# Graph attention and routed experts on one core: routing of four graphs in six parts, a second PSUM bank for V, and a new order of the drain

## What is computed

```python
def attention(x, adj):                       # on layernorm(x)
    q, k, v = x @ Wq.T, x @ Wk.T, x @ Wv.T   # 16 heads of 32
    p = softmax(q @ k.T * D ** -0.5 + adj + adj)
    return (p @ v) @ Wo.T

def experts(x):                              # on layernorm(x): 8 experts of 512 x 512, the best 2 count
    scores = maximum(x @ gate_W + gate_b, 1e-4)
    p = softmax(scores); top = top_k(p, 2)
    w = maximum(p, 0.1); w = w / w[top].sum(); comb = where(in_top, w, 0)
    return einsum(x @ expert_W + expert_b, comb) / 2

x = x + attention(layernorm(x), adj)
x = x + experts(layernorm(x))
```

## Time and profile before

| | |
|---|---|
| median of 3 runs | 1660.67 us (1660.43 to 1661.73) |
| the profiled execution | 1662.81 us; span from first to last instruction 1661.0 |
| PE busy | 1550.8 us, 93% |
| PEld busy | 1410.9 us, 85% |
| DVE busy | 1215.8 us, 73% |
| ACT busy | 955.9 us, 58% |
| POOL busy | 974.0 us, 59% |
| mean granted TensorE clock | 0.970 |

### The profile page before, as it was taken

The page is one execution under the profiler, slowest core; times in us unless marked ns, Lnnn a source line. Parts: engine busy times, 40 slices in busy tenths (PEclk is TensorE's granted clock), DMA queues, the critical chain, the costliest instruction groups (busy, mean ns, idle before and its releaser), DMA issues. The chain is left out here.

```text
span 1661.0 us, 45460 instructions
## 1 busy us (share of the span) xinstructions
PE 1550.8 (93%) x12808; PEld 1410.9 (85%) x12808; DVE 1215.8 (73%) x4952; ACT 955.9 (58%) x3129; POOL 974.0 (59%) x1788
## 2 busy tenths in 40 slices
PE   6999999999999999999999999966189999999996
PEld 6999999999999999999999999955167777777775
DVE  5578888888888888888888788877745555555554
ACT  4687777777777777777777777775111111111111
POOL 3255666566666666566665666556235565565655
PEclk9999999999999999999999999977599999999998
DMA  6787988789888888888887888794658898898886
GB/s 226 194 233 199 257 241 241 237 248 253 246 241 240 244 247 239 237 239 247 228 244 225 246 233 228 221 293 142 217 102 158 168 174 164 162 169 165 164 160 106
DMA packets 188629, 351.98 MB, mean 212 GB/s; under 512 B 20960, under 2 KB 30304, under 8 KB 188256
## 3 DMA queue, kind: packets, MB, share of 16 engines
q1 hardware_dynamic: 135520, 238.47, 51.7%
q0 software_dynamic: 29680, 69.55, 21.6%
q10 hardware_dynamic: 23184, 41.05, 8.0%
HBM read 189.48 MB, written 159.52 MB: 210 GB/s over the span
## 5 line engine op out<-in xcount | busy, mean ns | idle before, releaser
L678 ACT ACTIVATE prob<-prob,nmax 128x128 f32<-128x128 f32 x1024 | 398.8, 395 | 175.3 <-DVE amax L833 168.8
L1146 POOL TENSOR_TENSOR prob<-prob,rinv 128x512 f32<-128x512 f32 x256 | 261.4, 1042 | 241.3 <-DVE rinv L850 241.2
L829 DVE CUSTOM_DVE_ANT_0 prob<-ps_s,bias 128x128 f32<-128x128 f32 x1024 | 237.7, 287 | 142.1 <-PE ps_s L530 106.5
L1343 POOL DMA_INDIRECT out<-yt,token x135 | 211.6, 1567 | 196.3 <-DMA out<-yt,token 72.3
L1281 ACT ACTIVATE xgT_hi<-ps_x 128x512 fp32r<-128x512 f32 x135 | 80.7, 598 | 386.8 <-PE ps_x L1266 339.4
L1260 PE MATMUL ps_y<-we,xgT_hi 128*128 x540 | 260.8, 483 | 5.8 <-DVE xgT_lo L1300 5.8
L1261 PE MATMUL ps_y<-we,xgT_hi 128*128 x540 | 214.8, 398 | 0.0
L1262 PE MATMUL ps_y<-we,xgT_lo 128*128 x540 | 214.0, 396 | 0.0
L678 ACT ACTIVATION_READ_ACCUMULATOR prob<-prob,nmax 128x1 f32 x1024 | 196.7, 192 | 0.0
L833 DVE TENSOR_REDUCE amax<-prob 128x4 f32<-128x512 f32 x256 | 175.6, 686 | 8.9
L539 PE MATMUL ps_t<-const,prob 128*128 128x128 f32 x1024 | 164.8, 284 | 15.2 <-ACT pT L716 12.1
(11 more groups left out here) (191 smaller groups left out, 4770.4 us busy)
## 6 DMA issues: line engine op xcount, KB each, us to landing
ks<-kq_parts SPq DMA_DIRECT2D x192, 256.0 KB, 4.2
qs<-kq_parts SPq DMA_DIRECT2D x192, 256.0 KB, 6.3
xg<-x_lists ACTq DMA_DIRECT2D x135, 260.5 KB
xin<-x SPq DMA_DIRECT2D x64, 256.0 KB, 7.2
kq_parts<-kT_hi SPq DMA_DIRECT2D x32, 512.0 KB, 3.8
kq_parts<-kT_lo SPq DMA_DIRECT2D x32, 512.0 KB, 4.8
kq_parts<-qT_hi SPq DMA_DIRECT2D x32, 512.0 KB
kq_parts<-qT_lo SPq DMA_DIRECT2D x32, 512.0 KB
```

Of the source, the lines that this page charges most:

```text
L678: last = nc.scalar.activation(prob[:, r, c, h, :], prob[:, r, c, h, :], ACT.Exp, bias=nmax[:, r, i:i + 1], scale=-1.0, accum_out=rsum[:, r ...
L829: last = nc.vector.tensor_tensor_reduce(out=prob[:, r, c, h, :], in0=ps_s[c % 2][:, P * h:P * h + P], in1=bias[:, b % 4, :], scale=-1.0, s ...
L1146: tt(prob[:, r, q], prob[:, r, q], rinv[:, r, HC * q:HC * q + HC].unsqueeze(2).to_broadcast([P, HC, P]), ALU.mult)\
L1343: pool.indirect_dma_start(out=out, out_offset=bass.IndirectOffsetOnAxis(ap=token[:, m, :], axis=0), in_=yt[:, r, :], in_offset=None, compu ...
```

## The change

Routing goes by groups of four graphs (the last eight graphs by pairs). For group b to b + 3 the chain is cut in six parts on VectorE: scores (11 instructions) and first choice (4) at steps 0 and 2 of turn b + 7; second choice (7) at step 0 of turn b + 8; weigh (8) and combine (4) at steps 0 and 2 of turn b + 9; find (6) at step 0 of turn b + 10. ScalarE's eexp stands in turn b + 8, TensorE's counting, now eight matmuls for four graphs, at step 1 of turn b + 9. Graph b + a is scattered in turn b + 10 + a. V's right half of the pair's first graph goes to ps_o, of the second to ps_g. xn2 gets eight slots, gate_x six. In the drain the high and low parts of the experts stand elsewhere, GpSimd makes the statistics of graph 61 behind the last normalise and oT_lo, four pieces are left behind the table, and fourteen are made by VectorE in phase two, behind the low part of its second tile; TensorE waits for the pieces of its first three tiles by a value read from memory.

The diff, cut to its core:

```diff
+LATE = 18
...
+GROUPS = [(4 * q, 4) for q in range((B - 8) // 4)] + [(b, 2) for b in range(B - 8, B, 2)]
+STEPS = ("scores", "first", "second", "place", "exp", "weigh", "combine", "find")
...
+def plan():
+    at = {n: {} for n in STEPS}
+    for g, (b, n) in enumerate(GROUPS):
+        t = b + n
+        if n == 4 and GROUPS[g + 1][1] == 4:
+            when = (t + 3, 0), (t + 3, 2), (t + 4, 0), (t + 5, 1), (t + 4, 0), (t + 5, 0), (t + 5, 2), (t + 6, 0)
+        else:
+            when = (t + 2, 3), (t + 3, 0), (t + 3, 0), (t + 3, 2), (t + 3, 1), (t + 3, 2), (t + 4, 0), (t + 4, 0)
...
+        first_need = sb(top, "first_need", [1, RING], i32)
...
-        gate_x = sb("gate_x", [P, 8, E])
+        gate_x = sb("gate_x", [P, 6, E])
-        xn2 = sb("xn2", [P, 4, W])
+        xn2 = sb("xn2", [P, 8, W])
+        all_one = xn2[:, 0, 0:P]
-        pos = sb("pos", [P, 2, K, 2], i32)
+        pos = sb("pos", [P, 3, K, 4], i32)
...
-        G_V, G_P = ps_g[:, 0:D // 2 + E], ps_g[:, 3 * P:3 * P + 3 * E]
+        G_V, G_P = [ps_o[:, 0:D // 2 + E], ps_g[:, 0:D // 2 + E]], ps_g[:, 3 * P:3 * P + 5 * E]
-        O_W, O_S = ps_o[:, 0:DC * E], ps_o[:, DC * E:DC * E + E]
+        O_W, O_S = ps_t[:, 0:DC * E], ps_t[:, DC * E:DC * E + E]
...
-        HI_AT = [(B - 2, 1), (B - 2, 2), (B - 1, 1), (B - 1, 2), (B, 2), (B + 1, 3), (B + 3, 0), (B + 3, 1)]
-        LO_AT = {0: (B, 0), 1: (B, 2), 2: (B + 1, 0), 3: (B + 2, 0), 4: (B + 2, 2), 5: (B + 3, 0)}
+        HI_AT = [(B - 2, 1), (B - 2, 2), (B - 1, 1), (B + 1, 0), (B + 1, 2), (B + 2, 2), (B + 3, 0), (B + 3, 1)]
+        LO_AT = {(B - 1, 3): 2, (B, 0): 4, (B, 1): 2, (B + 2, 1): 6}
...
-                    if 2 * n + part:
-                        pe.wait_ge(v_done, 2 * n + part)
-                    if part == 0 and okp((t - 6) // 2):
-                        pe.wait_ge(place_step, PLACE * ((t - 6) // 2) + 1)
+                    if part == 0 and ok(t - 2):
+                        pe.wait_ge(oT_done, t - 1)
+                    if part == 1 and n >= 1:
+                        pe.wait_ge(v_done, 2 * n)
+                    if part == 1 and any(w < (t, c) for w in AT["place"]):
+                        pe.wait_ge(place_step, PLACE * max(g for w, g in AT["place"].items() if w < (t, c)) + 1)
...
+                    if b % 2 and ok(b + 3):
+                        pe.wait_ge(v_done, b + 4)
...
+            def places(g, t):
+                first, n = GROUPS[g]
+                pe.wait_ge(route_step, ROUTE * g + 16)
+                pe.wait_ge(v_done, min(B, t + 3))
...
+                mm(rows(G_P, 0, n + 1), tri[:, :], rows(sums, 0, n + 1), start=True, stop=False)
+                for i in range(1, n):
+                    mm(rows(G_P, i + 1, n + 1), ones[:, :], rows(sums, 1, n + 1 - i), start=False, stop=False)
+                for i in range(n):
+                    last = mm(rows(G_P, 0, 1), ones[:, :], rows(sums, i + 1, i + 2), start=False, stop=i == n - 1)
+                last.then_inc(place_full, 1)
...
-                    if b >= 8:
-                        act.wait_ge(x1_done, b - 7)
+                    if b >= 6:
+                        act.wait_ge(x1_done, b - 5)
...
-                if b >= 4:
-                    act.wait_ge(scattered[b % 4], 32 * (b // 4))
+                if b >= 8:
+                    act.wait_ge(scattered[b % 8], 32 * (b // 8))
...
+            def experts_lo(pieces):
+                for _ in range(pieces):
+                    e, i = divmod(made[0], DC)
+                    made[0] += 1
+                    dve.wait_ge(we_hi_done, e + 1)
                     own = slice(D * i, D * i + D)
                     tt(expert(e, 1)[:, own], expert(e, 1)[:, own].bitcast(f32), expert(e, 0)[:, own].bitcast(f32), ALU.subtract).then_inc(we_lo_done, 1)
...
+            ts(first_need[:, :], tab_f[:, 0, 0:RING], float(DC), float(DC), ALU.mult, ALU.add)
             link(nc.vector.tensor_copy(tab[:, :, :], tab_f[:, :, :]))
-            for e in range(len(LO_AT), E):
-                expert_lo(e)
+            experts_lo(LATE - made[0])
...
-                    if c == 0 and not odd and ok(t - 3):
+                    if c == 0 and not odd and ok(t - 3) and t < B:
                         second_rstd(t - 3)
...
                         tt(oT_lo[:, :, :], oT[:, :, :], oT_hi[:, :, :].bitcast(f32), ALU.subtract).then_inc(oT_lo_done, 1)
+                    if c == 0 and not odd and ok(t - 3) and t >= B:
+                        second_rstd(t - 3)
...
-                    if c == (3 - 2 * a if t < B else 3) and okp(p):
-                        scatter(p, a)
+                    if c == (3 if t >= B or not odd else 1):
+                        for b in range(B):
+                            g, a = GROUP_OF[b]
+                            if t == FOUND[g][0] + a:
+                                scatter(b)
...
+                        if not t.after(R):
+                            need = pe.value_load(v["first_need"][0:1, bass.ds(t.count(), 1)], min_val=DC, max_val=DC * E)
+                            pe.wait_ge(v["we_lo_done"], need)
...
+                    if (g, j) == (0, 0):
+                        for e, i in (divmod(piece, DC) for piece in range(LATE, DC * E)):
+                            hi, lo = (we[:, (2 * e + part) * DC * D + D * i:(2 * e + part) * DC * D + D * i + D] for part in range(2))
+                            tt(lo, lo.bitcast(f32), hi.bitcast(f32), ALU.subtract).then_inc(v["we_lo_done"], 1)
```

More of the change, by code:

```diff
@@ L49 @@
 C_ALL = C_DUM + E
+GROUPS = [(4 * q, 4) for q in range((B - 8) // 4)] + [(b, 2) for b in range(B - 8, B, 2)]
[8 more added lines that the diff above has]
+            when = (t + 2, 3), (t + 3, 0), (t + 3, 0), (t + 3, 2), (t + 3, 1), (t + 3, 2), (t + 4, 0), (t + 4, 0)
+        for name, w in zip(STEPS, when):
+            at[name][w] = g
+    return at
+AT = plan()
+FOUND = {g: w for w, g in AT["find"].items()}
+GROUP_OF = {b + a: (g, a) for g, (b, n) in enumerate(GROUPS) for a in range(n)}
 class Item:
@@ new lines, in landed, with combine @@
+            def landed(graphs):
+                for b in graphs:
+                    dve.wait_ge(scattered[b % 8], 32 * (b // 8 + 1))
+            def combine(g):
+                first, n = GROUPS[g]
+                link = chain(ROUTE * g, 22, route_step)
+                link(nc.vector.scalar_tensor_tensor(out=wgt[:, :, 0:n], in0=wgt[:, :, 0:n], scalar=1.0 / K,
+                                                    in1=wtot[:, 0:n].unsqueeze(1).to_broadcast([P, K, n]), op0=ALU.mult, op1=ALU.mult))
+                link(tt(comb_k[:, :, 0:n, :], mask[:, :, 0:n, :], wgt[:, :, 0:n].unsqueeze(3).to_broadcast([P, K, n, E]), ALU.mult))
+                landed(range(max(0, first - 8), first - 8 + n))
+                k = first % 8
+                tt(xn2[:, k:k + n, D + 1:W], comb_k[:, 0, 0:n], comb_k[:, 1, 0:n], ALU.add)
+                link(nc.vector.tensor_copy(xn2[:, k:k + n, D], const[:, C_TOK + first:C_TOK + first + n]))
@@ new lines, in find_places @@
+            def find_places(g):
+                _, n = GROUPS[g]
+                link = chain(PLACE * g, 0, place_step)
+                r = g % 3
+                old, new = fill[:, g % 2, :], fill[:, 1 - g % 2, :]
+                places = G_P.rearrange("p (a e) -> p a e", a=5)
+                dve.wait_ge(place_full, g + 1)
+                tt(place[:, 0:n, :], places[:, 1:n + 1, :], old.unsqueeze(1).to_broadcast([P, n, E]), ALU.add)
+                link(tt(new, places[:, 0, :], old, ALU.add))
@@ L1015, in _ @@
                         first_stats(t + 4 + c)
-                    p = (t - 6) // 2
-                    if not odd and okp(p):
-                        if c == 1:
-                            weigh(p)
-                            find_places(p)
-                    p = (t - 5) // 2
-                    if odd and okp(p):
-                        if c == 2:
-                            gate_scores(p)
-                        if c == 3:
-                            choose(p)
-                    for e, at in LO_AT.items():
-                        if at == (t, c):
-                            expert_lo(e)
-            dve.wait_ge(place_step, PLACE * (B // 2))
+                    if (t, c) in AT["scores"]:
+                        gate_scores(AT["scores"][t, c])
+                    if (t, c) in AT["first"]:
+                        choose_first(AT["first"][t, c])
+                    if (t, c) in AT["second"]:
+                        choose_second(AT["second"][t, c])
+                    if (t, c) in AT["weigh"]:
+                        weigh(AT["weigh"][t, c])
+                    if (t, c) in AT["combine"]:
+                        combine(AT["combine"][t, c])
+                    if (t, c) in AT["find"]:
+                        find_places(AT["find"][t, c])
+                    experts_lo(LO_AT.get((t, c), 0))
+            dve.wait_ge(place_step, PLACE * len(GROUPS))
```

224 lines of the change are left out of this document (100 added, 124 removed).

## The result

The changed kernel takes 1650.22 us (median of four runs, 1648.90 to 1650.76), the kernel before beside it 1660.55: ratio 0.9924, 95% interval 0.9912 to 0.9936. It is faster, but by a third of what I forecast: 1650.2 against 1630.3, outside my range of 1620 to 1648. The profiled execution has a span of 1649.0 us and 1650.75 in all, beside 1661.0 and 1662.8 before, so the two traces differ by 12.0.

The account below looks back on a forecast made before the run. TensorE's own work order was taken to bound 61 turns, so only its delays count. Terms -28.1 (turns), +1.5, +2.3, -6.5, -2.2, +2.6 sum to -30.4 us: 1630.3 against 1660.7, range 1620 to 1648.

Parts of the forecast that it names:

- A lump of four at step 0 of the odd turn: VectorE's longest routing part, 11 instructions, 2.1 us, fits a 4.9 us step beside 1.6 of maxima and 0.4 of reciprocals.
- the port rule: Drain: GpSimd and two-SBUF-input VectorE instructions exclude each other; the term to the last positions would then be -4.5 us.
- half of the gain: Rival, chance 0.16: VectorE's load slips in odd turns, output projection waits for the residual sum; 14 of 28 us, 1644.3.
- The even turns and the routing matmuls: Even turns fall to 16.9 to 17.0 us; eight routing matmuls add about 0.3 in every other odd turn.
- A bank for each graph: Even turns: separate banks for V's right halves remove V's second wait, 0.22 us for the copy out of ps_g.
- the 1.16 us: Price of routing per pair of turns on TensorE's path; taken back whole in 28 even turns, 32.4 us.
- The drain: GpSimd's new order delays ScalarE's xn of graph 61, then pT to the residual of graph 63: +2.3 us, bounds -2 and +5.
- To the last positions: From graph 63's residual to the last positions, six pieces and combine and find ahead: 14.6 us instead of 21.1, -6.5.
- Behind the table: End of phase one: VectorE makes four pieces there instead of eight: -2.2 us, bounds 0 and -2.4.
- Fourteen pieces: Phase two, ahead of the third xgT_lo: 8.6 us of pieces, partly in idle time, delay the first yt: +2.6, bounds 0 and +6.
- The end of the attention: Last scores: doubled late scatters lengthen the DMA queue ahead of graph 63's Q parts: +1.5 us, bounds 0 and 3.6.
- The slower rival, V in ps_o: Rival, chance 0.04: odd turn's product waits for ScalarE's copy out of ps_o, 2.7 us a pair, 81 us, 1711.

Follow-up runs that it names:

- run 1: Changed kernel with the 'scores' part of a group of four at step 1 of the even turn, not step 0 of the odd: 1642.6 us, ratio 0.9865.
- run 3: Changed kernel with the score tile of the groups of four in free columns of ps_g (PSUM) instead of SBUF: 1641.31 us, ratio 0.9866.
- Run 4: Changed kernel with the bank part alone undone, both right halves of V in ps_g again: 1649.98 us, ratio 0.9927.
- Run 6: Changed kernel with GpSimd's old order in the drain, second_rstd ahead of normalise and oT_lo: 1645.71 us, ratio 0.9891.
- run 10: Changed kernel with 'scores' at step 1 of the even turn, GpSimd's old drain order and LATE = 32, no piece in phase two: 1641.65 us, ratio 0.9882.
- run 11: The changed kernel measured again, unaltered: 1649.38 us, ratio 0.9913.

## Why the prediction was wrong

The direction and the mechanism of the gain were right, the size was not. By its own steps:

*A lump of four at step 0 of the odd turn: the step that failed.* "The longest lump, 11 instructions (2.1 us), stands at step 0 of an odd turn ...: it fits." It took 4.6. Count and step price were right: away from GpSimd the part takes 1.97 us (run 1), and with its scores in PSUM 2.01 (run 3). What I put at nothing was the overlap with GpSimd's products, 2.6 us. I priced the chain by comb_k, 192 ns, which stands after GpSimd's products. In the same view stood the warning (VectorE by line, 200 to 1000 us, of the kernel before; busy, mean ns of one):
```profile
L929 DVE TENSOR_TENSOR em<-eexp,mask 128x16 f32<-128x16 f32 x23 | 13.1, 568 | 0.0
```
half the size of comb_k, three times as long: it stood beside oT_lo and ended with it (at 598.29 and 598.26 in turn 32). I brought the port rule in for the drain and never asked what GpSimd does at each of the places the parts were moved to. What followed is the wait of my rival "half of the gain", to which I gave 0.16: the output projection waits for the sum with the residual. That rival named lack of room, not GpSimd, as the reason, and it priced 14 us. Runs 1 and 3 put the waits at 0.67 us in every other pair, 8.8 us over 26 pairs. The pair without them, 33.21 against 33.17, is 1.1 more; the last 0.6 of the 10.5 lies in the first and last groups (my 28.1 also counts the pair of turn 60, which the stretch to turn 60 does not) and was not taken apart.

*The even turns and the routing matmuls* were right: 16.97 us, and 0.28 in every other odd turn. *A bank for each graph* I credited with a part of the 1.16 us. Run 4 shows that it brings nothing beside the new routing.

*The drain*, +2.3 with a bound of +5, measured +4.9. The chain I named is the one that happened. The term was mis-sized: xn of graph 61 came 14.4 us behind its residual where I had 11.4. Half of that is second_rstd, which took 5.0 us beside VectorE's six pieces and not 3.5; I had taken stretched steps into account for graph 63 alone. The rest is normalise of graph 63, which started 6.1 us behind that residual and not 4.3 (GpSimd stood 1.01 us for VectorE's rinv), though it was 0.5 shorter. Run 6 gives this part of the loss as 3.7.

*To the last positions*, -6.5, measured -5.4: between the sum and what I wrote for the port rule, -4.5. VectorE waits 0.82 us for off of graph 63 behind its pieces.

*Behind the table*, -2.2, measured +0.2, just outside my bound of 0. Before, the first load came 1.0 us behind VectorE's last piece; after, 3.5 us behind it. With VectorE out of the way another chain ended phase one: the load comes 15.4 to 16.2 us behind the last positions in every run with LATE up to 23, against 15.3 before. SyncE, after its DMAs, stands 2.9 us more for TensorE's sequencer, and I had counted only the landing of the last scatter. That wait names no cause: in run 10, where VectorE's pieces end the phase, the same wait is 9.2 us, so the sequencer may pass on the lateness of another engine. What sets the 15.4 us was not tried.

*Fourteen pieces*, +2.6, measured +2.3: the room of six microseconds was right (ten pieces free, run 10), the closeness of the sum is in part luck. The pieces cost 1.7; the other 0.6 stands without any piece. The value reads of first_need, which I put at nothing, are the likely cause, not a tested one.

*The end of the attention*, +1.5, measured +0.1: two executions of the changed kernel differ by 1.5 us in this stretch (run 11), so one profile of each kernel cannot tell +0.1 from +1.5. Whether the doubled scatters hold up the last loads stays open.

The gap of 18.4 us between the sum and the traces is 10.5 in the turns, 2.5 at the start, 2.6 and 1.1 in the drain, 2.4 behind the table and 0.9 at the end, less 1.4 and 0.3. The slower rival, V in ps_o, did not show: no wait for that copy in any turn.

## What to carry to other kernels

When work is moved on VectorE, look at GpSimd's timeline at the new place before pricing it: an instruction of 0.2 us took up to 1.1 there. Price a small operation by its own row, and take a mean three times that of its peers as a question. Where an operand can live in PSUM, the meeting costs nothing. When a change has several parts that act on one wait, test each alone and without the others: here one was worth 0.26 us a pair by itself and nothing beside its neighbour, and a third was a loss that the whole hid.

## What the runs showed of the hardware

A VectorE multiplication with one SBUF tensor input, SBUF to SBUF in f32 (128x8, four of them), waited for GpSimd's product like the two-input form: 2.31 us. A cast from SBUF to SBUF (128x8) waited too: 0.95 in place of 0.17. A reciprocal (0.18), a reduce (128x512, 0.69 as elsewhere) and an instruction with one input in PSUM and one in SBUF (0.63 for four) did not. The lock works both ways: six VectorE pieces took 6.46 us in place of 3.70 beside normalise and oT_lo, and normalise took 2.94 in place of 2.04.

TensorE's granted clock in the first turns varies between executions of one program. Ahead of the fall in the changed kernel (0.72 in the stretch of 46 to 50 us) TensorE had stood 2.10 us for a load; but in run 6 it stood 2.09 us there and was granted 1.00, so that wait alone does not decide. In the stretch of 60 to 66 us it was granted 0.50, 0.60 or 0.84 of full speed, and turn 1 started up to 4.4 us apart. At this level, a quarter of a per cent of the time, one profiled execution of each kernel is not enough to price a part.
